# adaLN FFN kernel: pair 2's first round by seven products, weight differences moved into the head and pair 1, reordered queues

## What is computed

```python
att = softmax(gelu(gelu(cond @ W0 + b0) @ W1 + b1) @ W2 + b2)       # (64, 8)
agg_w = einsum('bk,koi->boi', att, weight)                           # (64, 64, 64)
h = einsum('boi,bih->boh', agg_w, x) + (att @ bias_k)[:, :, None]    # x: (64, 64, 1024)
scores = h @ gate_w.T + gate_b                                       # 4 ranks: 8, 16, 32, 64
out = h @ W.T + b + h @ A[:r].T @ B[:, :r].T                         # r by the largest score
return x + out
```

## Time and profile before

| | us |
|---|---|
| median of 3 runs | 458.8 (458.18 to 459.92) |
| the profiled execution | 458.18 |
| its span in the trace | 456.3 |
| PE busy | 450.4 |
| DVE busy | 343.8 |
| ACT busy | 181.4 |

### The profile page before, as it was taken

How to read it: one execution, slowest core, us unless ns; L and a number is a source line. 1 busy time by engine, 2 the same in 40 slices (tenths; PEclk the granted TensorE clock), 3 DMA queues, 4 the chain that set the end, 5 groups by cost and what they waited for, 6 DMA issues and landing times.

```text
span 456.3 us, 10477 instructions
## 1 busy us (share of the span) xinstructions
PE 450.4 (99%) x3510; PEld 445.8 (98%) x3510; DVE 343.8 (75%) x889; ACT 181.4 (40%) x415; POOL 19.4 (4%) x46
## 2 busy tenths in 40 slices
PE   9999999899999999999999999999999999999997
PEld 7999999899999999999999999999999999999997
DVE  4887988799586876958687695868769586876945
ACT  5654554455243343524334342433334243342511
POOL 1010000010000000000000000000000000100000
PEclk9999999999999999999999999999999999999999
DMA  7973560711608053250805235080523408052202
GB/s 273 344 277 54 145 227 1 239 46 52 232 1 278 6 188 97 88 195 0 281 1 194 88 90 192 0 278 4 201 81 108 174 5 277 0 190 95 92 2 93
DMA packets 23773, 59.18 MB, mean 130 GB/s; under 512 B 6862, under 2 KB 8834, under 8 KB 23684
## 3 DMA queue, kind: packets, MB, share of 16 engines
q1 hardware_dynamic: 23508, 58.78, 39.0%
q10 hardware_dynamic: 240, 0.07, 0.1%
HBM read 40.69 MB, written 18.15 MB: 129 GB/s over the span
## 4 chain that ended last, share of the span: by engine, by line
PE 96%; DVE 3%; ACT 1%; issue 0%; POOL 0%; ACTq 0%; POOLq 0%
PE p_p L1071 74%; PE p_o L1089 4%; PE p_o L1091 4%; PE p_o L1109 3%; PE p_o L1090 3%; PE p_o L1108 3%; PE p_p L1115 1%; PE p_p L1136 1%; PE p_p L1097 1%; PE p_o L1136 1%; DVE wl L716 1%; DVE w_raw L722 1%; DVE zl L792 0%; DVE aggw L776 0%; DVE prod L773 0%
## 5 line engine op out<-in xcount | busy, mean ns | idle before, releaser
L1071 PE MATMUL p_p<-wh,xh 128*128 128x274 f32 (+1 forms) x880 | 256.6, 292 | 0.0
L1071 PE MATMUL p_p<-wh,xl 128*128 128x274 f32 (+1 forms) x880 | 254.2, 289 | 0.0
L1071 PE MATMUL p_p<-wl,xh 128*128 128x272 f32 (+1 forms) x864 | 250.5, 290 | 0.0
L1071 PEld LDWEIGHTS p_p<-wh,xh 128*128 128x128 f32 x880 | 166.5, 189 | 0.4 <-issue 0.4
L1071 PEld LDWEIGHTS p_p<-wh,xl 128*128 128x128 f32 x880 | 166.7, 189 | 0.1
L1071 PEld LDWEIGHTS p_p<-wl,xh 128*128 128x128 f32 x864 | 163.0, 189 | 0.1
L579 ACT ACTIVATE zh<-sv 128x274 fp32r<-128x274 f32 (+1 forms) x56 | 24.3, 433 | 95.0 <-DVE sv L804 95.0
L811 DVE TENSOR_TENSOR xin<-p_o,xin 128x274 f32<-128x274 f32 (+2 forms) x128 | 52.0, 418 | 2.7 <-PE p_o L1109 1.9
L557 ACT ACTIVATE xh<-s_raw 128x512 fp32r<-128x512 f32 x60 | 36.3, 628 | 17.1 <-DVE s_raw L759 16.4
L579 ACT ACTIVATE zh<-p_p 128x272 fp32r<-128x272 f32 (+1 forms) x44 | 17.5, 398 | 60.7 <-PE p_p L1071 59.0
L766 DVE TENSOR_TENSOR xl<-s_raw,xh 128x512 fp32r<-128x512 f32 x60 | 40.9, 682 | 0.1
(11 more groups left out here) (140 smaller groups left out, 508.4 us busy)
## 6 DMA issues: line engine op xcount, KB each, us to landing
xin<-in_x SPq DMA_DIRECT2D x32, 512.0 KB, 4.0
raw<-in_xt SPq DMA_DIRECT2D x31, 512.0 KB, 5.2
out<-xin SPq DMA_DIRECT2D x30, 512.0 KB, 5.9
w_raw<-in_w SPq DMA_DIRECT2D x8, 274.0 KB, 7.0
w_raw<-in_w SPq DMA_DIRECT2D x8, 272.0 KB, 6.0
g_aggw<-aggw_all SPq DMA_DIRECT2D x8, 128.0 KB, 2.4
aggw<-g_aggw SPq DMA_DIRECT2D x15, 64.0 KB, 5.0
out<-xin SPq DMA_DIRECT2D x4, 137.0 KB, 2.1
```

The lines of the kernel that those rows point to most:

```text
L1071: last = nc.tensor.matmul(o[:, 0:W[r]], a, m, start=start and p == 0, stop=stop and p == 2, skip_group_check=True)
```

## The change

TERMWISE becomes 1, so pair 2's first round runs by seven products too. Round 0's weight combinations, made and split in pair 2 before, are now made in the head (sum R11), in pair 1's second round (sums R12, R22, R21, rest of R22) and in pair 2's first round (rests of R11, R12, R21). SP loads x's first tile in other pieces. In the head some of ACT's and DVE's work changes places, and two calls of keep_busy(2) go. The last piece is written out: its two zh matmuls and its LoRA pair stand ahead of the zl matmul.

```diff
--- before.py
+++ after.py
@@ -40,6 +40,5 @@
 T_SUMS = (R11, R12, R22, R21)
+T_LOWS = (R22, R11, R12, R21)
 
-T_LOWS = ((R22, R12, R21, R11), (R22, R11, R12, R21))
-
-TERMWISE = 2
+TERMWISE = 1
 
@@ -221,2 +220,3 @@
         s_raw_first_in = sem("s_raw_first_in")
+        s_raw_rest_in = sem("s_raw_rest_in")
         s_stored = [sem(f"s_stored{i}") for i in range(4)]
@@ -357,3 +357,5 @@
                 if m == 0:
-                    sp.dma_start(raw[:, 0, FIRST * P:], xt[0][:, FIRST * P:]).then_inc(s_raw_in[0], 16)
+                    sp.dma_start(raw[:, 0, FIRST * P:HB], xt[0][:, FIRST * P:HB]).then_inc(s_raw_rest_in, 16)
+                if m == 1:
+                    sp.dma_start(raw[:, 0, HB:], xt[0][:, HB:]).then_inc(s_raw_in[0], 16)
                 if m == 3:
@@ -618,2 +620,4 @@
             z_hi(0, 0, 0, Z11)
+            w_hi(10)
+            w_hi(11)
             act.wait_ge(s_clear, 5)
@@ -623,4 +627,2 @@
             nc.scalar.activation(b_h.bitcast(F32R), b_raw, ACT.Copy).then_inc(s_b_hi, 1)
-            w_hi(10)
-            w_hi(11)
             cs_hi(1)
@@ -652,6 +654,7 @@
 
-                two = is_pair(i, j, TERMWISE)
+                two = is_pair(i, j, TERMWISE + 1)
                 if early(i, j, 0):
                     a_hi(i, j, A21)
-                a_hi(i, j, A22)
+                if not two:
+                    a_hi(i, j, A22)
                 z_hi(i, j - 1, 1, Z21)
@@ -666,5 +669,11 @@
                 bd_hi(i, j, 1)
+                if two:
+                    t_hi(0, R12)
                 if not one:
                     s_hi(i, j, S4)
+                if two:
+                    a_hi(i, j, A22)
                 z_hi(i, j, 0, Z11)
+                if two:
+                    t_hi(0, R21)
                 if one:
@@ -682,9 +691,4 @@
                     s_hi(i, j, S4)
-                if two:
-                    t_hi(0, R22)
-                    t_hi(0, R12)
                 z_hi(i, j, 0, Z21)
 
-                if two:
-                    t_hi(0, R21)
                 snapshot(i, j, 1)
@@ -692,4 +696,2 @@
                     a_hi(i, j + 1, A11)
-                if two:
-                    t_hi(0, R11)
                 z_hi(i, j, 1, Z11)
@@ -699,2 +701,4 @@
                 z_hi(i, j, 1, Z22)
+                if one:
+                    t_hi(0, R22)
                 if not last:
@@ -702,2 +706,4 @@
                 z_hi(i, j, 1, Z12)
+                if one:
+                    t_hi(0, R11)
 
@@ -729,3 +735,3 @@
                     ks = slice(2 * h, 2 * h + 2)
-                    dve.wait_ge(s_th[r], 2 * T_LOWS[r].index(n) + h + 1)
+                    dve.wait_ge(s_th[r], 2 * T_LOWS.index(n) + h + 1)
                     nc.vector.tensor_tensor(wl[r][:, T_OF[n], ks, :], w_raw[r][:, n, ks, :],
@@ -850,3 +856,3 @@
             nc.vector.tensor_tensor(logit[:, :], ps_logit, b2r[:, :], ALU.add).then_inc(s_sm, 1)
-            dve.wait_ge(s_raw_in[0], 16)
+            dve.wait_ge(s_raw_rest_in, 16)
             rest = slice(FIRST * P, HB)
@@ -861,2 +867,3 @@
             w_lo(1)
+            dve.wait_ge(s_raw_in[0], 16)
             nc.vector.tensor_copy(xh[:, A12, :], raw[:, 0, HB:H]).then_inc(s_x0h, 1)
@@ -890,3 +897,3 @@
                 w_lo(3 + n)
-                if n == 1:
+                if n == 2:
                     dve.wait_ge(s_rows_mm, 1)
@@ -915,2 +922,3 @@
             nc.vector.tensor_copy(kern_h[:, :], kern_s[:, :]).then_inc(s_kern_hl, 1)
+            w_lo(8)
             cs_lo(1)
@@ -921,5 +929,4 @@
             nc.vector.tensor_tensor(b_l.bitcast(F32R), b_raw, b_h, ALU.subtract).then_inc(s_b_lo, 1)
-            w_lo(8)
-            w_lo(9)
             z_lo(0, 0, 0, Z12)
+            w_lo(9)
             w_lo(10)
@@ -939,2 +946,3 @@
             t_sum(1, R11, R12, R11)
+            t_sum(0, R11, R12, R11)
             cs_lo(3)
@@ -966,3 +974,4 @@
                 z_lo(i, j - 1, 1, Z21)
-                a_lo(i, j, A22)
+                if not two:
+                    a_lo(i, j, A22)
                 if one:
@@ -976,6 +985,6 @@
                     residual(i, j - 1, 1, Z12)
-                if not early(i, j, 0):
                     add(i, j, 0, SU2)
-                if not one and not two:
                     s_lo(i, j, S1)
+                if two:
+                    t_lo(0, R11)
                 bd_lo(i, j, 1)
@@ -983,7 +992,5 @@
                     residual(i, j - 1, 1, Z21)
-                if two:
-                    t_sum(0, R11, R12, R11)
-                    t_sum(0, R12, R22, R12)
-                elif not one:
                     s_lo(i, j, S3)
+                if two:
+                    t_lo(0, R12)
                 z_lo(i, j, 0, Z11)
@@ -992,8 +999,4 @@
                     s_lo(i, j, S2)
-                elif two:
-                    dve.wait_ge(s_tsum[0], 4)
-                    t_sum(0, R22, R22, R11)
                 else:
                     s_lo(i, j, S4)
-                if not early(i, j, 0):
                     add(i, j, 0, SV)
@@ -1002,4 +1005,4 @@
                 if two:
-                    dve.wait_ge(s_tsum[0], 6)
-                    t_sum(0, R21, R21, R22)
+                    a_lo(i, j, A22)
+                    t_lo(0, R21)
                 if one:
@@ -1007,10 +1010,5 @@
                     t_lo(1, R12)
-                if not early(i, j, 0):
+                else:
                     add(i, j, 0, S12)
                 z_lo(i, j, 0, Z12)
-                if two:
-                    s_lo(i, j, S1)
-                    t_lo(0, R22)
-                    t_lo(0, R12)
-                    s_lo(i, j, S3)
                 if one:
@@ -1025,8 +1023,6 @@
                 add(i, j, 1, SU2)
-                if two:
-                    t_lo(0, R21)
-                    s_lo(i, j, S4)
-                    t_lo(0, R11)
                 if not last:
                     a_lo(i, j + 1, A11)
+                if one:
+                    t_sum(0, R12, R22, R12)
                 z_lo(i, j, 1, Z11)
@@ -1035,2 +1031,5 @@
                 add(i, j, 1, SV)
+                if one:
+                    dve.wait_ge(s_tsum[0], 4)
+                    t_sum(0, R22, R22, R11)
                 if not last:
@@ -1050,2 +1049,5 @@
                     x_sum(i, j + 1, S4)
+                if one:
+                    dve.wait_ge(s_tsum[0], 6)
+                    t_sum(0, R21, R21, R22)
                 residual(i, j, 1, Z11)
@@ -1053,2 +1055,4 @@
                     s_lo(i, j + 1, S2)
+                if one:
+                    t_lo(0, R22)
 
@@ -1157,4 +1161,2 @@
                     if kk % 2 == 0:
-                        if at < 2:
-                            keep_busy(2)
                         pe.wait_ge(s_wl, at + 1)
@@ -1275,3 +1277,3 @@
                     if first:
-                        pe.wait_ge(s_tl[r], 2 * T_LOWS[r].index(n) + 2)
+                        pe.wait_ge(s_tl[r], 2 * T_LOWS.index(n) + 2)
 
@@ -1336,5 +1338,15 @@
             last = (PAIRS // 2 - 1, 1)
-            for n in (Z12, Z21):
-                mix(*last, 1, n)
-                lora(*last, 1, n)
+            mix(*last, 1, Z12)
+            lora(*last, 1, Z12)
+
+            cols, mine = COLS[1][Z21], slice(P, 2 * P)
+            o, zs = p_o[:, OBANK[Z21], 0:W[1]], slice(0, W[1])
+            pe.wait_ge(s_zh, piece(*last, 1, Z21))
+            pe.wait_ge(s_y, piece(*last, 1, Z21 - 4))
+            nc.tensor.matmul(o, bd[:, 1, 0, :], zh[:, 1, zs], start=True, stop=False)
+            nc.tensor.matmul(o, bd[:, 1, 1, :], zh[:, 1, zs], start=False, stop=False)
+            nc.tensor.matmul(o, ut_hl[:, mine], bt_h[:, cols], start=False, stop=False)
+            nc.tensor.matmul(o, ut_h1[0:ROWS, mine], bt_l[0:ROWS, cols], start=False, stop=False)
+            pe.wait_ge(s_zl, piece(*last, 1, Z21))
+            nc.tensor.matmul(o, bd[:, 1, 0, :], zl[:, 1, zs], start=False, stop=True).then_inc(s_lora, 1)
```

4 lines of the change are left out of this document (2 added, 2 removed).

## The result

The changed kernel is slower. Its median is 463.48 us (462.14 to 466.25, 6 runs), that of the kernel before in the same session 458.67 (458.18 to 459.92, 6 runs); the ratio is 1.0106, with a 95% interval of 1.0086 to 1.0127. The forecast was 459.2, with a range from 456.0 to 460.9. The ratios of this document leave out four single runs of later sessions that took far longer than the others of their kernel: three of the kernel before (879 to 1119 us) and one in experiment 3 (467.27).

What follows compares the result with a forecast made beforehand. PE, busy 450.4 of 456.3 us, was taken to bound the kernel. Terms -0.91 - 0.89 - 0.50 - 3.03 + 5.50 + 0.21 = +0.4 on the median of 458.8 gave 459.2 us, range 456.0 to 460.9.

Steps and rivals of the forecast that it cites:

- Pair 2: Pair 2's first round: -3.03 us for eight units becoming seven and a hole gone, +5.50 for new waits.
- the new waits: Pair 2's first round: PE waits for weight differences at P6, P5, P7, P4: 1.62, 1.08, 1.19, 1.61; sum 5.50 us.
- From mark to mark: From P7 of pair 1's second round to P7 of pair 2's: 32.2 us instead of 29.5.
- lateness of DVE: Pair 2's first round: DVE hardly pauses from 70 to 94 us; s_lo(S2) starts 1.77 later, delaying the weight differences.
- The head: Start of the kernel: dropped dummies -0.91 us, z_lo(Z12) no longer awaited -0.89, moved weight sums 0.
- The z_lo hole: Head: the mixing matmul at 28.16 no longer waits for z_lo(Z12); -0.89 us, bounds 0.4 to 0.89.
- The dummies: Head: two dropped pairs of keep_busy matmuls start the second 20-matmul unit earlier; -0.91 us, 0.4 less if the clock rises later.
- What is queued behind: SP's queue in pair 2: loads behind its later wait for a_lo(A22) still land in time; cost 0, thinnest cover 0.7 us.
- Rival 2: Four holes in pair 2's first round drop PE's clock, slowing the matmuls behind; 463.0 us; chance 0.12.
- The last piece: End of the kernel: four of five matmuls no longer wait for z_lo, and residual and store move along; -0.50 us.
- Rival 1: Pair 2's weight differences half hidden, DVE being less behind: 456.4 us (chance 0.17), or 453.5 without new waits (0.06).
- Rival 3: Head gives nothing: reordered loads and dropped dummies only let PE wait for w_lo sooner; 460.1 us; chance 0.10.

Runs made afterwards that it cites:

- experiment 3: k_rows loaded by four 16-row DMAs: changed kernel 465.39 us, kernel before with head's edits 461.49, changed with classical pair 2 460.72; changed kernel with x load whole 463.86.
- the repaired queue: SP issues g_kern stores ahead of xin loads and the g_rows wait, k_rows loads ahead of column-sum stores: changed kernel 459.70 us, kernel before 457.53.
- pair 2's part alone: Kernel before with only pair 2's seven products in its first round and the moved weight sums and rests: 461.76 us, ratio 1.0055.
- the second half of the head's edit: Kernel before with only the first x load in two and the two pairs of dummy matmuls gone: 460.55 us, ratio 1.0044.

## Why the prediction was wrong

**Pair 2: right in mechanism, place and size.** The four rows that end the new waits, in the changed kernel:

```profile
87.19 0.36 PE L1075 MATMUL p_p<-wh,xh 128*128 128x272 f32 x1 [1.56 <-DVE wl L737]
...
91.88 0.36 PE L1075 MATMUL p_p<-wh,xh 128*128 128x272 f32 x1 [0.80 <-DVE wl L737]
...
94.59 0.36 PE L1075 MATMUL p_p<-wh,xh 128*128 128x272 f32 x1 [0.96 <-DVE wl L737]
...
99.78 0.36 PE L1075 MATMUL p_p<-wh,xh 128*128 128x272 f32 x1 [1.56 <-DVE wl L737]
```

From the matmul before each, less one spacing, they are 1.73, 0.96, 1.13 and 1.71, together 5.5; forecast 1.62, 1.08, 1.19 and 1.61, together 5.50. (By the text's own times the first two are 81.34 - 79.77 = 1.57 and 86.08 - 85.05 = 1.03; it adds 0.05 to each without saying why.) From mark to mark 32.31, forecast 32.2.

The text called this lateness of DVE; the runs make it sharper. Only the first wait is a backlog, which less work ahead of it removes. The others are order. DVE's rows ahead of P5's difference in the changed kernel:

```profile
89.43 0.43 DVE L810 TENSOR_TENSOR su<-p_p,su 128x272 f32<-128x272 f32 x1
89.78 0.68 DVE L772 TENSOR_TENSOR xl<-s_raw,xh 128x512 fp32r<-128x512 f32 x1
90.38 1.35 DVE L737 TENSOR_TENSOR wl<-w_raw,wh 128x544 fp32r<-128x544 f32 x2
```

The difference needs nothing that PE computes, but stands behind an addition that does (89.43, SU2). So DVE starts each one only when PE has come to within a unit of needing it, however early DVE is.

**The head: right in direction, too large, and by how much depends on the clock's start.** In the two given profiles the mark moved by 1.25, forecast 1.80. The z_lo hole went as said (0.87 of 0.89). The dummies gave 0.59 up to the end of the second 20-matmul unit (13.41 for 14.00) in place of 0.91, since the clock rose at 10.15, not at 9.62; that is the 0.4 to 0.9 that the text allowed. 0.20 of it went again at 15.09, where PE now waits for the attention weights.

```profile
10.15 0.29 PE L1075 MATMUL p_p<-wl,xh 128*128 128x272 f32 x1
...
15.09 0.29 PE L1140 MATMUL p_o<-b12l,ones_r 128*128 128x272 f32 x1
15.51 0.30 PE L1179 MATMUL p_o<-attt,bk 8*64 8x32 f32 x4
```

Both of these profiles have a late rise of the clock. Where it rises early the dropped dummies have given nothing by the attention matmuls: PE waits for ACT's weights and for the attention weights, whose matmul starts at 14.60 and 14.80 with the old head (before with the repaired queue, pair 2's part alone) and between 15.05 and 15.65 in all profiles with the new head and a rise ahead of 8 us, but for one at 16.53. With the repaired queue the mark stands at 38.54 with the old head and at 37.56 to 38.41 with the new one, a gain of 0.1 to 1.0.

**The step that failed: the head's 1.80 was booked as a gain of the end.** Alone, the head made the kernel slower, by a ratio of 1.0107, some 4.9 us. The text asks after w_lo(2), after the z_lo and after the column sums, all on DVE, and never what PE meets next that no engine makes. That is k_rows, by the program the first thing behind round 1 of pair 0 that comes through DRAM. "What is queued behind" followed SP's queue in pair 2, where the change moved a wait, and not in the head, where it moved two loads and DVE's work. Before, PE met k_rows without a wait, so it stood in no list; its margin had to be worked out from its packets (last one at 40.46, PE there at 42.47, and about 1.5 from last packet to matmul in the runs that waited, as 42.30 to 43.76 and 43.84 to 45.33).

**Rival 2 named the right mechanism in the wrong place.** Pair 2's four holes, each 1.1 to 1.9 from matmul to matmul, left the clock at its upper level in every profile; spacings behind them are 0.13 again from the second matmul on. The one hole of 2.73 in the head lowered it for 10 us in the profiled run. What the text cites there of the Trainium skill (TensorE: Matmul & The Clock Gate, "HAM oscillation") held for the place that nobody had looked at, and not for the four holes. That section speaks of idle gaps longer than any of these five, so "by that rule this change would be slower" read more into it than it says; the hole of 2.73 shows that a shorter one can be enough. The forecast of 463.0 for this rival is near the result by chance.

**The last piece: right on PE, two thirds of it at the end.** The last matmul starts at 461.28, 0.63 behind the LoRA matmul at 460.65; before it was 1.15 behind the earlier trace rows. That is 0.52, forecast 0.50. From the last matmul's start to the end of the span are 3.2 us where there were 3.0, so 0.3 arrives.

```profile
460.65 0.29 PE L1113 MATMUL p_o<-bt_l,ut_h 69*128 69x274 f32 x1
...
461.28 0.29 PE L1351 MATMUL p_o<-zl,bd 128*128 128x274 f32 x1
```

**Rivals 1 and 3.** Rival 1 was refuted: the differences weren't hidden. Rival 3, that the reordered loads and dropped dummies only let PE wait sooner, was refuted for the given profile, where the dummies gave 0.59; where the clock rises early it is what happens.

**Open.** Why the g_rows stores land a microsecond or more later with any of the head's edits. Gate rows, which follow that landing, go out at 26.72 and 27.03 in the two profiles with the old head and the old queue, and between 27.75 and 29.89 in the ten with any part of the new head and the old queue. The queue is full from 8 to 30 us at up to 400 GB/s, and by 14 us the changed kernel has moved 3.68 MB where before has moved 3.91. One profile for each kernel doesn't tell how much of this is chance. The kernel before with the repaired queue has them at 28.31 with the old head, but there they stand behind the g_kern stores.

## What to carry to other kernels

When PE is made to arrive earlier, list everything it meets next, and above all what it has so far met without a wait: a transfer with half a microsecond of margin is in no list of waits, and shaving the path ahead of it turns it into a hole. Where a store and a load through DRAM precede it, issue the store as soon as its data exists, not behind loads that nobody awaits yet. Before a difference of half a microsecond between two profiles is put down to an edit, look whether it is there ahead of anything that the edit touches. And put work that needs nothing from PE ahead of work that does in an engine's order: three of four waits here were a difference of two constants standing behind an addition.

## What the runs showed of the hardware

- What the granted clock did behind a hole of PE, measured from matmul to matmul: the four of 1.1 to 1.85 us in 13 us left it at 2.4 GHz in every profile, and so did one of 2.41 at 28.43 us (the second half of the head's edit). Behind those of 2.51, 2.73, 3.4 to 4.4 and 5.4 us it fell to 1.2 GHz, and behind a wait of 2.9 us filled with dummy matmuls it did not. How long it stayed low did not follow the length of the hole: by the granted clock about 10 us behind that of 2.73, 3.4 behind those of 2.51 and 3.4 to 4.0, 6.8 behind those of 4.4 and 5.4.
- When the clock first rose: between 4.5 and 10.2 us, in 19 profiles with nearly the same head. It was worth 1.29 us at 12.7 us and 0.7 at 39, and the granted clock of the profile doesn't show it.
- Loads of 8 rows run on half of the sixteen DMA engines, at 73 GB/s (77 in before, from 35 to 40 us); a load with a leading broadcast of two on two, at 51.
- A GpSimd addition of 128x544 takes 1.83 us, and a DVE addition with both inputs in SBUF beside it 1.82 in place of 0.71. Moving 5.8 us of work to GpSimd cost DVE more than it freed: with eight instructions fewer it was busy 347.8 us instead of 346.1.
